# An attention and expert layer on one core: transpositions in both side banks, split rows in two buffers, no late split, the shared down projection in fp32

## The reference, cut to what matters

```python
xn = layernorm(x)                                   # x is 8 batches x 256 tokens x 128
x  = x + attn(xn) + ffn(xn)

def attn(x):                                        # 16 heads of 64, 2 null keys per head
    q  = (layernorm(x)*norm_g + norm_b) @ Wq
    k, v = split(x @ Wkv)
    q, k = l2norm(q)*q_scale, l2norm(k)*k_scale     # the null keys and values are put in front
    sim = 8 * q @ k.T + slope[h] * -|j - i|         # causal
    return softmax(sim) @ v @ Wout

def ffn(x):
    shared = (silu(x @ sg_w.T) * (x @ su_w.T)) @ sd_w.T
    top-2 of 8 experts by sigmoid(x @ router_w.T + bias), weights normed to sum 1
    return shared + sum of weight * expert(x)       # each expert: silu(gate) * up, then down
```

## Time and profile before

| | before |
|---|---|
| median of 3 runs | 491.92 us (491.72 to 493.71) |
| the profiled execution's own time | 492.31 us |
| its span in the profile | 490.6 us |
| TensorE busy | 423.7 us, 86% of the span |
| VectorE busy | 363.6 us, 74% |
| ScalarE busy | 358.9 us, 73% |
| GpSimd busy | 319.9 us, 65% |

### The profile page before, as it was taken

One profiled execution on the slowest core, in us unless ns is written; L12 is line 12 of the kernel. 1 busy time (PEld: TensorE's weight loads), 2 busy tenths in 40 slices (PEclk: granted clock), 3 DMA queues, 4 the chain that ended last, 5 costly groups with the idle time before them and its releaser, 6 DMA issues.

```text
span 490.6 us, 10747 instructions
## 1 busy us (share of the span) xinstructions
PE 423.7 (86%) x2809; PEld 306.4 (62%) x2809; DVE 363.6 (74%) x1419; ACT 358.9 (73%) x1098; POOL 319.9 (65%) x492
## 2 busy tenths in 40 slices
PE   4746807999997997999899899989999998999995
PEld 3734405777775775767666676766667676767663
DVE  5699604666644996798789779878978986997894
ACT  3354703666667986889897798989779798979874
POOL 3748779800005789498867959886795988778150
PEclk9969856999999999899999999999999999999999
DMA  8961111222220000000001000000100000010010
GB/s 236 321 227 33 54 53 49 76 82 81 79 62 16 1 18 6 3 23 21 3 1 35 11 1 24 21 3 2 37 8 2 22 23 3 1 38 7 2 43 13
DMA packets 29739, 21.37 MB, mean 44 GB/s; under 512 B 3528, under 2 KB 27376, under 8 KB 29552
## 3 DMA queue, kind: packets, MB, share of 16 engines
q1 hardware_dynamic: 26816, 16.46, 11.4%
q0 software_dynamic: 2048, 4.20, 2.9%
q10 hardware_dynamic: 816, 0.03, 0.1%
HBM read 12.41 MB, written 8.26 MB: 42 GB/s over the span
## 4 chain that ended last, share of the span: by engine, by line
PE 35%; POOL 24%; DVE 19%; issue 11%; ACT 7%; DMA 2%; ACTq 1%; DVEq 0%; POOLq 0%; SPq 0%
POOL slot_x L416 7%; PE bank L971 5%; DVE arena_b L900 5%; POOL rnorm L426 5%; PE bank L1190 4%; PE bank L1120 4%; PE bank L972 4%; PE bank L973 4%; POOL arena_b L506 4%; DVE arena_b L915 3%; PE bank L1111 3%; DVE arena_b L877 3%; POOL rpow L429 2%; POOL arena_b L442 2%; PE bank L1134 2%
## 5 line engine op out<-in xcount | busy, mean ns | idle before, releaser
L676 ACT ACTIVATE arena_b<-arena_b,nmx 128x130 f32<-128x130 f32 (+1 forms) x256 | 114.7, 456 | 17.4 <-DVE nmx L900 14.8
L900 DVE CUSTOM_DVE_ANT_0 arena_b<-bank,bias 128x130 f32<-128x130 f32 (+1 forms) x256 | 81.1, 354 | 37.5 <-ACT arena_b L676 20.9
L915 DVE TENSOR_SCALAR arena_b<-arena_b,rden 128x130 f32<-128x130 f32 (+1 forms) x256 | 78.5, 354 | 4.5
L429 POOL TENSOR_TENSOR rpow<-ssm,mhalf 128x8 f32<-128x8 f32 x32 | 52.9, 1653 | 36.2 <-DVE ssm L888 35.5
L1111 PE MATMUL bank<-ident,arena_b 128*128 128x128 f32 x384 | 67.4, 285 | 5.6 <-DVE arena_b L915 5.6
L442 POOL TENSOR_TENSOR arena_b<-arena_b,rnorm 128x512 f32<-128x512 f32 x64 | 66.9, 1045 | 5.0
L1120 PE MATMUL bank<-arena_a 64*128 64x130 f32 (+1 forms) x512 | 60.2, 354 | 0.8 <-ACT arena_a L637 0.8
L1111 PEld LDWEIGHTS bank<-ident,arena_b 128*128 128x128 f32 x384 | 44.1, 142 | 24.9 <-DVE arena_b L915 14.4
L884 DVE TENSOR_REDUCE ssq<-arena_b 128x8 f32<-128x512 f32 x64 | 43.7, 683 | 13.2 <-ACT arena_b L614 12.4
L426 POOL TENSOR_TENSOR rnorm<-ssm,mhalf 128x8 f32<-128x8 f32 x32 | 52.5, 1641 | 0.0
L676 ACT ACTIVATION_READ_ACCUMULATOR arena_b<-arena_b,nmx 128x1 f32 x256 | 50.8, 199 | 0.0
(11 more groups left out here) (209 smaller groups left out, 1030.3 us busy)
## 6 DMA issues: line engine op xcount, KB each, us to landing
slot_x<-probT SPq DMA_DIRECT2D x3, 832.0 KB, 8.6
...
```

The costliest lines, as they stand in the source:

```text
L429: gp.tensor_tensor(rpow[:, j, :], ssm[:, j, :], mhalf[:, 0:HEADS // 2], ALU.pow).then_inc(g.pw, 1)
L676: sc.activation(prob[:, (HEADS * b + h) % RP, c], sim[h % 2][:, c], ACT.Exp, scale=-1.0, bias=nmx[:, h % HEADS, t:t + 1], accum_out=den[:, ...
L900: ve.tensor_tensor_reduce(out=sim[h % 2][:, c], in0=bank[h % 2][:, c], in1=bias[:, c], scale=-SLOPES[h], scalar=3e38, op0=ALU.add, op1=ALU ...
L915: ve.tensor_scalar(pr, pr, rden[:, h % HEADS, t:t + 1], None, ALU.mult).then_inc(g.pn, 1)
```

## The change

1. **Split rows in two buffers.** `xs1` and `xs2` are rings of two. The query split of batch b + 2 is made at step 3 of batch b (before: of batch b + 1 at its step 0). The key split stays at step 1, and since its buffer now survives a batch, the batch's own values and shared expert read it: `xs_late` and its two instructions go.
2. **The shared down projection in fp32.** `sd` is one fp32 tensor, TensorE multiplies `hs` itself with two fp32 matmuls, and the four GpSimd instructions for `hss` go.
3. **The side table.** The next batch's transpositions (half c = 0) were in bank 7 at steps 10 to 13. They are now (9, bank 5), (10, bank 5), (10, bank 7) and (14, bank 7). The key projection of step 13 moves from bank 5 to bank 7, and the values of steps 14 and 15 to steps 13 and 14. TensorE waits, ahead of the scores of head 0, until bank 7 has been emptied.
4. **Order within a step.** On TensorE, jobs of bank 5 stand ahead of "out" and jobs of bank 7 behind it; the null matmul (L1127) goes to the start of step 5. On VectorE, at odd steps, what belongs to bank 5 (sums of squares among it) goes ahead of the row maxima. On ScalarE, the copy of `yT` at step 6 goes behind the exponentials.

The diff, cut to what acts in the attention stage (setup code changes only with the buffers' new indices):

```diff
-        sd = [sb("sd_hi", [P, 2, DIM], F32R), sb("sd_lo", [P, 2, DIM], F32R)]
+        sd = sb("sd", [P, 2, DIM])
...
-        xs1, xs2 = ([carve_r(SEQ), carve_r(SEQ)] for _ in range(2))
+        xs1, xs2 = ([[carve_r(SEQ), carve_r(SEQ)]] for _ in range(2))
         mxT = [[carve_r(P), carve_r(P)] for _ in range(RH)]
         rt[0] = 4 * SEQ
+        for ring in (xs1, xs2):
+            ring.append([carve_r(SEQ), carve_r(SEQ)])
-        hss = [carve_r(2 * I), carve_r(2 * I)]
...
-        xs_late = [sb(f"xs_late{i}", [P, SEQ], F32R) for i in range(2)]
...
         JOBS = [[(1, "next", "kq", 0, 1, 0), (2, "prev", "pn", 0, 0, 0), (4, "next", "kq", 0, 1, 1), (5, "next", "kq", 0, 0, 0),
-                 (6, "next", "kq", 0, 0, 1), (7, "prev", "yt", 0, 0, 0), (8, "own", "v", 1, 0, 1), (11, "next", "kq", 1, 1, 1),
-                 (12, "next", "kq", 1, 0, 0), (13, "next", "kq", 1, 0, 1), (14, "next", "v", 0, 0, 0), (15, "next", "v", 0, 0, 1)],
+                 (6, "next", "kq", 0, 0, 1), (7, "prev", "yt", 0, 0, 0), (8, "own", "v", 1, 0, 1), (9, "next", "tr", 0, 1, 1),
+                 (10, "next", "tr", 0, 0, 0), (11, "next", "kq", 1, 1, 1), (12, "next", "kq", 1, 0, 0), (13, "next", "v", 0, 0, 0),
+                 (14, "next", "v", 0, 0, 1)],
                 [(0, "own", "tr", 1, 1, 0), (1, "own", "tr", 1, 1, 1), (2, "own", "tr", 1, 0, 0), (3, "own", "tr", 1, 0, 1),
                  (4, "own", "v", 1, 0, 0), (5, "own", "sh", 0, 0, 0), (7, "next", "kq", 1, 1, 0), (8, "own", "sh", 1, 0, 0),
-                 (10, "next", "tr", 0, 1, 0), (11, "next", "tr", 0, 1, 1), (12, "next", "tr", 0, 0, 0), (13, "next", "tr", 0, 0, 1)]]
+                 (10, "next", "tr", 0, 1, 0), (13, "next", "kq", 1, 0, 1), (14, "next", "tr", 0, 0, 1)]]
...
+            def split_for_queries(n):
+                xs, cols = xs2[n % 2], bass.ds(n * SEQ, SEQ)
+                gp.tensor_copy(xs[0], xn2T[:, cols]).then_inc(g.xhi, 1)
+                pool.wait_ge(g.xhi, 2 * n + 1)
+                gp.tensor_tensor(xs[1], xn2T[:, cols], xs[0].bitcast(F32), ALU.subtract).then_inc(g.xlo, 1)
+
             def entry(part, b, steps=range(HEADS)):
                 whose = PARTS[part]
                 for s in steps:
-                    if s < 2 and "next" in whose and part != "ready":
-                        xT, xs = ((xn2T, xs2), (xn1T, xs1))[s]
+                    if s == 0 and part == "first":
+                        split_for_queries(1)
+                    if s == 1 and "next" in whose and part != "ready":
...
-                                pool.wait_ge(filled[i], count("ahead", i) + count("ready", i))
-                        settled(pool)
-                        gp.tensor_copy(xs[0], xT[:, bass.ds(nb * SEQ, SEQ)]).then_inc(g.xhi, 1)
-                        pool.wait_ge(g.xhi, 2 * nb + s + 1)
-                        settled(pool)
-                        gp.tensor_tensor(xs[1], xT[:, bass.ds(nb * SEQ, SEQ)], xs[0].bitcast(F32),
-                                         ALU.subtract).then_inc(g.xlo, 1)
-                    if s in (7, 10) and "own" in whose:
-                        c = (7, 10).index(s)
-                        pool.wait_ge(g.sh_h, 2 * b + c + 1)
-                        if part != "first":
-                            pool.wait_ge(g.shd, b)
-                        settled(pool)
-                        gp.tensor_copy(hss[0][:, c * SEQ:(c + 1) * SEQ], hs[:, c, :]).then_inc(g.sh_hi, 1)
-                        pool.wait_ge(g.sh_hi, 2 * b + c + 1)
-                        gp.tensor_tensor(hss[1][:, c * SEQ:(c + 1) * SEQ], hs[:, c, :],
-                                         hss[0][:, c * SEQ:(c + 1) * SEQ].bitcast(F32), ALU.subtract).then_inc(g.sh_lo, 1)
-                    if s == 2 and "own" in whose:
-                        settled(pool)
-                        gp.tensor_copy(xs_late[0][:], xn1T[:, bass.ds(b * SEQ, SEQ)]).then_inc(g.late_hi, 1)
-                        pool.wait_ge(g.late_hi, b + 1)
-                        settled(pool)
-                        gp.tensor_tensor(xs_late[1][:], xn1T[:, bass.ds(b * SEQ, SEQ)], xs_late[0][:].bitcast(F32),
-                                         ALU.subtract).then_inc(g.late_lo, 1)
+                        xs, cols = xs1[nb % 2], bass.ds(nb * SEQ, SEQ)
+                        gp.tensor_copy(xs[0], xn1T[:, cols]).then_inc(g.xhi, 1)
+                        pool.wait_ge(g.xhi, 2 * nb + 2)
+                        gp.tensor_tensor(xs[1], xn1T[:, cols], xs[0].bitcast(F32), ALU.subtract).then_inc(g.xlo, 1)
...
+                    if s == 3 and "next" in whose and nb + 1 < BATCH:
+                        for _, _, (kind, c, w, t, i, n) in (x for lag in range(1, HEADS) for x in behind(part, b, s, lag)):
+                            if (kind, c, w, t) == ("kq", 1, 1, 1) and part != "first":
+                                pool.wait_ge(filled[i], n + 1)
+                        split_for_queries(nb + 1)
...
-                    if s == 6 and "prev" in whose:
-                        act.wait_ge(g.oread, PAIRS * b)
-                        act.wait_ge(g.fin, b)
-                        sc.activation(yT, bank[6][:, 0:SEQ], ACT.Copy).then_inc(g.yev, 1)
                     h = head_at(part, s, 1)
                     if h is not None:
                         if part != "first" or h >= RP:
@@ -676,6 +664,11 @@
                             sc.activation(prob[:, (HEADS * b + h) % RP, c], sim[h % 2][:, c], ACT.Exp, scale=-1.0,
                                           bias=nmx[:, h % HEADS, t:t + 1],
                                           accum_out=den[:, h % HEADS, t:t + 1]).then_inc(g.exp, 1)
+                    if s == 6 and "prev" in whose:
+                        act.wait_ge(g.oread, PAIRS * b)
+                        act.wait_ge(g.fin, b)
+                        sc.activation(yT, bank[6][:, 0:SEQ], ACT.Copy).then_inc(g.yev, 1)
...
+                    done = behind(part, b, s, 1)
+                    for job in done:
+                        if job[2][4] == 0:
+                            side_out(*job)
                     if s % 2 == 1:
                         row_maxima(part, b, s)
+                    for job in done:
+                        if job[2][4] == 1:
+                            side_out(*job)
                     h = head_at(part, s, 3)
-                    for job in behind(part, b, s, 1):
...
-                    ins = three(side[i][:], [x[:, tt] for x in (xs2 if w else xs1)],
+                    ins = three(side[i][:], [x[:, tt] for x in (xs2 if w else xs1)[nb % 2]],
...
                 if kind == "v":
-                    if c:
-                        pe.wait_ge(g.late_lo, b + 1)
-                    else:
-                        pe.wait_ge(g.xlo, 2 * nb + 2)
-                    ins = three(side[i][:], [x[:, tt] for x in (xs_late if c else xs1)],
+                    pe.wait_ge(g.xlo, 2 * (b if c else nb) + 2)
+                    ins = three(side[i][:], [x[:, tt] for x in xs1[(b if c else nb) % 2]],
...
+                    if s == 5 and "prev" in whose:
+                        pe.wait_ge(g.pn_lo, b)
+                        te.matmul(bank[6][:, 0:SEQ], unull[:], pnT[:], start=False, stop=False)
...
+                        if h == 0 and part != "first":
+                            pe.wait_ge(left[1], jobs_until(part, b, 1, 0))
...
                     for job in todo:
-                        side_job(job, b)
-                    if s == 5 and "prev" in whose:
-                        pe.wait_ge(g.pn_lo, b)
-                        te.matmul(bank[6][:, 0:SEQ], unull[:], pnT[:], start=False, stop=False)
+                        if job[4] == 0:
+                            side_job(job, b)
                     h = head_at(part, s, 6)
                     if h is not None and h % 2:
                         p = h // 2
...
                         te.matmul(bank[6][:, 0:SEQ], wo[:, p % PAIRS, :], oT[p % 2][:], start=p == 0,
                                   stop=p == -1).then_inc(g.oread, 1)
+                    for job in todo:
+                        if job[4] == 1:
+                            side_job(job, b)
                     if s == 13 and "own" in whose:
-                        pe.wait_ge(g.sh_lo, 2 * b + 2)
+                        pe.wait_ge(g.sh_h, 2 * b + 2)
                         for c in range(2):
-                            ins = three(bank[6][:, 0:SEQ], [x[:, c, :] for x in sd], [x[:, c * SEQ:(c + 1) * SEQ] for x in hss],
-                                        False, False)
-                        ins.then_inc(g.shd, 1)
+                            te.matmul(bank[6][:, 0:SEQ], sd[:, c, :], hs[:, c, :], start=False, stop=False)
```

50 lines of the change are left out of this document (23 added, 27 removed).

## The result

| | time, us | ratio to before, 95% |
|---|---|---|
| before, 6 runs beside it | 492.62 (491.04 to 493.87) | |
| after, 6 runs | 485.57 (484.58 to 486.97) | 0.9859 (0.983 to 0.9888) |

The kernel is 1.4% faster, 7.05 us. The forecast was 16.3 us, and 485.57 lies outside its range of 470 to 483. The direction was right; more than half of the gain is missing.

The account below looks back on a forecast made before the run. TensorE was taken as nearest to the bound, kept waiting by GpSimd's split and VectorE's normalisation. Terms summed to 20.4 us gained, 4.1 lost, 16.3 net: 491.92 to 475.6 us, range 470 to 483.

Parts of the forecast that it names:

- Order on VectorE, and `yT`: Odd steps: sums of squares ahead of row maxima, and the later `yT` copy at step 6, cost nothing.
- the shared port: Rival: VectorE steps 7 to 10, one more instruction blocked by GpSimd per batch, 4.7 us, giving 480.3; chance 0.08.
- failure sign: Prediction fails if the period stays above 41.2 us, or if scores of head 0 show a wait.
- The stall at step 1: Step 1, batches 1 to 6: TensorE's wait for GpSimd's split (L460) goes whole, 10.0 us gained.
- the clock: Batch 1: TensorE's granted clock no longer falls to 0.68 after the long wait, 1.6 us gained.
- Transpositions at steps 9 and 10, and step 11: Moved transpositions fill TensorE's waits and head 6's normalisation is freed, 4.7 us; second step 10 job fills step 11, 2.2.
- Bank 7 behind "out": Step 3: "out" runs while TensorE's transposition would wait for ScalarE to empty bank 7, 1.9 us gained.
- The down projection: Shared down projection: two fp32 matmuls take 0.86 us against 0.72 for six fp32r, 1.1 us lost over eight batches.
- The new wait at step 13: Step 13: values wait for ScalarE to empty bank 5 after the key projection, 0.3 us a batch, 1.8 lost.
- Friction: Whole period: small unseen waits with ScalarE and VectorE nearly full, 0.2 us a batch, 1.2 us lost.
- The guard at step 0: Rival: scores of head 0 wait until bank 7 is emptied, giving 498 at 4.9 us of lateness; chance 0.04.

Follow-up runs that it names:

- the first run: The changed kernel with VectorE's old order at odd steps (row maxima ahead of all side work): 475.42 us, ratio 0.9667, period 40.43.
- part 1 alone: The kernel before with only the split rows in two buffers and no late pair; table, orders and down projection as before: 482.61 us, ratio 0.9812.
- the whole reversal: The changed kernel with VectorE's old order, TensorE's bank 7 jobs ahead of "out" again, and two GpSimd multiplications held: 479.07 us, ratio 0.9719.

## Why the prediction was wrong, and where it was right

**The step that failed** is "Order on VectorE, and `yT`", which said that sums of squares ahead of odd row maxima "let GpSimd start its powers earlier, where it has slack now. I cost both at nothing". GpSimd has slack; VectorE, on which its multiplications then fall, has next to none in steps 5 to 8. This term covers the whole of the missing gain: undone it gives 475.42 us for the 475.6 forecast, and with the order kept and the multiplications held, 476.18. What it put at nothing costs 1.05 us in each period, or 485.57 - 475.42 = 10.2 us in all, 9.4 by the ratios to the runs beside each (of the 9.5 us between the two profiled spans, 6.3 lie in the six stretches from step 2 to step 2, 1.7 ahead of them, and 1.6 ahead of the first scores).

The prediction had the mechanism among its rivals ("the shared port") and gave it 0.08 and one blocked instruction of 0.78 us a period, 480.3 us in all. The changed kernel has two more of them in each period on the busy stretch, for 0.63 + 0.88 = 1.51 us. Of that the first run's list gives 0.12 at its own L881 (0.29 for 0.17) and 0.31 at the residual, where it takes 2.05 us (290.32 in its mid batch) and after 1.74 (at 297.03); what is left, 1.08 us, is the 1.05 by which the periods differ. The sentence "the rows cannot tell where the multiplications will fall" was true, but what follows from it is a wider range and a larger chance, not a term of nothing. Its failure sign was named rightly: the period stays above 41.2 us, "which means that ScalarE or VectorE took over". It was VectorE.

The other terms, by the runs:

- *The stall at step 1* (10.0, with the clock 1.6): part 1 alone takes the five periods from 213.44 to 206.34 us, 1.42 each where 1.24 + 0.17 were read off, and the stretch ahead of them, with the stall and the clock of batch 1, from 47.53 to 43.41, 4.1 where 2.65 + 0.17 + 1.6 were; the time falls by 9.5 us where 11.6 were forecast. TensorE's granted clock over the start of batch 1 is 1.00 in the changed kernel, the level of 2.4 GHz, where it was 0.68:

```profile
192.15:200.88 8.73, 8.73 (x71) 6.42 (x70) 7.87 (x32) 8.29 (x27) 5.89 (x12) 1.00 0.01 3
```

- *Transpositions at steps 9 and 10, and step 11* (4.7 + 2.2, 1.15 a period): the table undone costs 0.48 a period. That run keeps the freed pair of `hss` (0.36), so 0.79 were at stake in it; 0.3 of them did not show. The wait at step 10 is 0.45 in the first run, for "about 0.3".
- *Bank 7 behind "out"* (1.9, 0.32 a period): the wait at step 3 is worth 0.37. The 0.52 to 0.55 of the whole reversal hold another 0.17 at step 8, which need not be the order's.
- *The down projection* (1.1 against): TensorE pays what was said, 0.86 us (from 311.07 to 311.93), for 0.72. The freed GpSimd pair was counted above, 0.36; 0.36 - 0.14 = 0.22 a period, and 0.20 were measured. In the time it is worth 4 us, and not six times 0.2, since without it batch 1 falls into the 1.40 us wait and batch 0 is 1.0 us longer.

```profile
311.07 1.02 PE L1140 MATMUL bank<-arena_b,sd 128*128 128x256 f32 x4
311.93 0.49 PE L1109 MATMUL bank<-ident,arena_b 128*128 128x128 f32 x3
```

- *The new wait at step 13* (1.8 against): it never came, in this kernel or another. The emptying of bank 5 is hidden. These 0.3 us a period about make up for the 0.3 that the table did not give.
- *Friction* (1.2 against) has no single place. The kernel without multiplications shows what all collisions with them still cost the first run: 40.43 - 39.68 = 0.75 us a period.
- *The guard at step 0* (rival, 0.04): TensorE has no wait there in batches 1 to 7.

That the sum of the others met the first run within 0.2 us owes something to chance, since what part 1 and the table gave less was made up by step 13 and by bank 7. And the first run is not the kernel that was forecast: that one has the new order.

Left open: why each kernel's period settles at just that distance between GpSimd and VectorE, and why VectorE's L908, whose record starts 0.03 us ahead of the multiplication's in two of the kernels, is the one that is held.

The version to keep is the change with the multiplication in quarters (473.38 us), or with the old order and the residual's multiplication held (474.04); the intervals of the two overlap. Both beat before and after.
